# Two layers of cross-attention and FFN on one core: the first layer's softmax sums made on VectorE by 32-row transposes and additions, in place of TensorE products with ones

## Chip, cores and metric

One core of one Trainium2 chip runs one launch of the kernel. The metric is device time in microseconds, the median of the runs of a kernel; smaller is better.

## The reference, cut to what matters

All data is float32. x and the context hold 16 batches of 64 tokens with 512 features. The change touches the first layer's attention only, 32 query heads in 8 key-value heads of 128:

```
x = x + _L0_xattn_ref(_layernorm(x), ctx, ctx, mask, Wq, Wk, Wv, Wo)   # the change is in here
x = x + _L0_ffn_ref(_layernorm(x), A, B, Wr)                          # gated low-rank experts
x = x + _L1_xattn_ref(_layernorm(x), ctx, Wq, Wk, Wv, Wo)             # 16 heads of 96
x = x + _L1_ffn_ref(_layernorm(x), W, bias, A, Bf, coeffs, scales)

# in _L0_xattn_ref, per batch and head:
logits = 30.0 * jnp.tanh(einsum(q, k) * ATTN_MULT / 30.0)
logits = jnp.where(mask, logits, -1e30)
weights = jax.nn.softmax(logits, axis=-1)       # exp(logit) / sum over the 64 context tokens
attn = einsum(weights, v);  return attn @ Wo
```

## The kernel before, in words

The program is one hand-written list of steps, made by `plan()`. Every engine walks the same list and does its own part of each step, in that order, so the list is each engine's queue. Semaphores join the engines. Large products are made from float32r halves ("h" and "l"), three products for each, 12 for a tile of 512 columns.

The first layer runs in 16 units u = 0 to 15. A unit is half of the batches (8 of 16) for one key-value head, with its four query heads. Unit u does this:

- `burst(u)`: the attention's own products, together. `d0(u-2)` multiplies weights with V in two halves h, each with two PSUM tiles; `sum0(u-1)` makes sums of exponentials; `b0(u)` makes the logits of this unit, context tokens on the partitions (two batches of 64 on 128 rows), 1024 columns of queries.
- ScalarE then takes tanh and exp, GpSimd multiplies with the mask (`keep`, semaphore `masked`). The result is E0, 128x1024, in `Eb` for even u and in `pTb` for odd u.
- four projections `q0(u+1, n)` of the next unit, each with a rope: three VectorE operations (L1249, L1250, L1252, the last of which frees the PSUM bank) and an addition on GpSimd (L903). `b0(u+1)` waits for the last of these additions. In even units each is followed by `split` steps for weights: a copy by ScalarE and a subtraction by GpSimd (L880).
- four output products `e0(u-2, c)`, which VectorE adds to x (L1163). After the second stands `norm0(u-1)`: VectorE multiplies E0 with `rsum`, the reciprocal sums (L1271). `d0` of that unit waits for it.
- `k0`, the next key-value head's projection with its own rope (until unit 13), and in units 0 to 3 two V tiles, `v0`.

The sums: the context tokens lie on partitions, so TensorE multiplies E0 with `ones` (128x32), eight products of 128 columns (L1534, two instructions each) into one bank. VectorE takes the reciprocal (L1267, 128x256), SyncE writes it to the DRAM tensor `recs` with two DMAs (L827), waits for their landing, and reads it back into `rsum`, broadcast over the partitions, with two DMAs of 256 KB (L832). SyncE's queue also issues the weight loads (L804), three splits ahead of their use, in list order.

PSUM tiles without a fixed bank take the next of a ring of six banks (0, 1, 4, 5, 6, 7). A tile waits until the sixth tile before it has been read.

Around the last units the list is: unit 15 with k1(0, 0, 0), e0(13, 0), e0(13, 1), norm0(14), e0(13, 2), e0(13, 3), the splits of the last four output weights wo0 28 to 31; then k1(0, 0, 1), burst(16) with d0(14), k1(1, 0, 0), and e0(14, 0). The load of wo0 31 stands behind the split of wo0 28.

Of the kernel before, what the change touches and what calls it, by code (L numbers as in the profile page):

```python
# [7 lines left out]
NU = 16  # L8
# [54 lines left out]
def plan():  # L63
    p = Plan()
# [61 lines left out]
    def burst(u):  # L126

        if 0 <= u - 2:
            for h in range(2):
                for w in range(2):  # L130
                    tile("d0", u - 2, h, w)
                step("d0", u - 2, h)
        if 0 <= u - 1 < NU:
            stage("sum0", u - 1)
        if u < NU:
            for h in range(2):
                tile("b0", u, h, bank=2 + h)
            step("b0", u)
# [78 lines left out]
    for u in range(NU):  # L217

        def queries(n):
            if u + 1 < NU:  # L220
                q0(u + 1, n)
                if u % 2 == 0 and u + 2 < NU:
                    split("wq0", 2 * u + 4 + n)

        def outputs(c):
            if u >= 2:
                e0(u - 2, c)

        j, hf = u // 2 + 1, u % 2
        pr, m = u // 4 + 1, u % 4  # L230
        if u == 0:
            for c in range(2):
                split("wv0", 1, c)
        burst(u)
        if u == NU - 1:
            k1(0, 0, 0)
            split("wk1", 2, 0)
        queries(0)
        queries(1)
        for c in range(2):  # L240
            outputs(c)
            if u in (4, 6):
                split("wvq", u - 4 + c)
        if u:
            norm0(u - 1)
        queries(2)
        outputs(2)
        queries(3)
        outputs(3)

        wo = [2 * u - 2 + n for n in range(4)] if u % 2 else []

        def output_weight():
            if wo:
                split("wo0", wo.pop(0))

        output_weight()
        if u and j < 8:
            k0(j, hf)
            if hf and j + 1 < 8:  # L260
                split("wk0", j + 1)
        output_weight()
        if pr < 2:
            for i in range(2):
                v0(pr, 2 * m + i)
                output_weight()

        for i in {8: (0, 1, 2), 9: (3, 4, 5), 10: (6, 7)}.get(u, ()):
            vq(i)
            output_weight()  # L270
        while wo:
            output_weight()
        if u == NU - 3:
            split("wk1", 0, 0)
        if u == NU - 2:
            split("wk1", 1, 0)
            split("wv1", 0)
# [259 lines left out]
def program(nc, a, out):  # L537
# [18 lines left out]
    with ExitStack() as ctx:  # L556
# [4 lines left out]
            return ctx.enter_context(nc.semaphore(name))  # L561


        rec = sb("rec", [128, 2, 128])

        tab = sb("tab", [128, 272])
        rope = tab[:, 0:128].rearrange("p (a n) -> p a n", a=2)
        ident = tab[:, 128:256]
        mask8 = tab[:, 256:272].bitcast(u8)
        keep = sb("keep", [128, 64])  # L570
        ones = sb("ones", [128, 32])
        many = sb("many", [128, 64])
        mv = sb("mv", [128, 8, 2])
        sm = sb("sm", [128, 2, 2, 8])
# [49 lines left out]
        V1h = sb("V1h", [128, 2, 2, 2, 96], f32r)  # L624
        V1l = sb("V1l", [128, 2, 2, 2, 96], f32r)
        ropeq = sb("ropeq", [128, 2, 64])
        recs = nc.dram_tensor("recs", (2, 2, 4, 128), f32, kind="Internal").ap()
        lowtri = sb("lowtri_sb", [128, 16])
        coef = sb("coef_sb", [128, 4])
        wcol = sb("wcol", [128, 2])  # L630
# [54 lines left out]
        s_out_rec, s_in_rec = sem("rec_out"), sem("rec_in")  # L685
# [104 lines left out]
        def sync_program(e):  # L790
            sp = Lane(e)
            for kind, *k in steps:
# [20 lines left out]
                elif kind == "ctx_load":  # L813
                    h, = k
                    for c in range(4):
                        src = a["ctxT"][c * 128:(c + 1) * 128, 512 * h:512 * h + 512]
                        e.dma_start(cst[c][h], src).then_inc(s_ldc[4 * h + c], 16)
                elif kind == "x":
                    i, = k
                    e.dma_start(xs[:, i, :], a["x"][i * 128:(i + 1) * 128, :]).then_inc(s_ldx[i], 16)  # L820
                elif kind == "sum0":
                    u, = k
                    sp.wait_ge(*read("sum0", u))
                    if u:
                        sp.wait_ge(s_in_rec, 32 * u)
                    for bb in range(2):
                        e.dma_start(recs[bb].rearrange("h g x -> g h x"), rec[16 * bb:128:32, :, :]).then_inc(s_out_rec, 16)  # L827
                    sp.wait_ge(s_out_rec, 32 * (u + 1))
                    if u:
                        sp.wait_ge(s_nrm, u)  # L830
                    for bb in range(2):
                        e.dma_start(rsum[64 * bb:64 * bb + 64, :],  # L832
                                    recs[bb].rearrange("h g x -> (h g x)").unsqueeze(0).broadcast_to([64, 1024])
                                    ).then_inc(s_in_rec, 16)
                elif kind == "ffn_load":
                    sp.wait_ge(*done("b0", 15, 1))
                    e.dma_start(aw_sb, a["aw"].rearrange("p (k n) -> p k n", k=4)).then_inc(s_aw, 16)
                    e.dma_start(bcat_sb, a["bcat"]).then_inc(s_bcat, 16)
                    e.dma_start(lowtri[:, :], a["lowtri"]).then_inc(s_low, 16)
                elif kind == "weff_load":  # L840
                    sp.wait_ge(*done("b1", 7))
                    e.dma_start(w1T[:, :, :], a["w1"].rearrange("p (k n) -> p k n", k=4)).then_inc(s_w1, 16)
                elif kind == "factor_load":
                    sp.wait_ge(*done("b1", 7))
                    e.dma_start(coef[:, 0:2], a["coef"]).then_inc(s_coef, 16)
                    e.dma_start(coef[:, 2:4], a["scl"]).then_inc(s_scl, 16)
                    for c in range(2):
                        e.dma_start(ab_sb[:, c, :], a["a1"][c]).then_inc(s_ab[c], 16)
# [18 lines left out]
        def gpsimd_program(e):  # L867
            pool = Lane(e)
            for kind, *k in steps:
# [33 lines left out]
                    e.tensor_tensor(dst, dst, tmp, ALU.add).then_inc(s_radd)  # L903
                elif kind == "consts":
                    e.memset(pTb[:, 0, 0:128], 1.0).then_inc(s_one)
                    e.memset(ones[:, :], 0.0).then_inc(s_one)
                    pool.wait_ge(s_one, 2)
                    for r in range(2):
                        e.memset(ones[64 * r:64 * r + 64, 16 * r:16 * r + 16], 1.0).then_inc(s_one)
                        pool.wait_ge(s_one, 3 + r)  # L910
                elif kind == "ctx":
                    h, c = k
                    if h:
# [244 lines left out]
        def vector_program(e):  # L1158
# [6 lines left out]
            for kind, *k in steps:  # L1165
# [94 lines left out]
                    e.tensor_scalar(many[:, :], PB[b][:, 0:64], 1.0, None, ALU.min).then_inc(free[b])  # L1260
                elif kind == "sum0":
                    u, = k
                    b = bank_of("sum0", u)
                    dve.wait_ge(*done("sum0", u))
                    if u:
                        dve.wait_ge(s_out_rec, 32 * u)
                    e.reciprocal(rec[:, :, :], PB[b][:, 0:256].rearrange("p (h x) -> p h x", h=2)).then_inc(free[b])  # L1267
                elif kind == "norm0":
                    u, = k
                    dve.wait_ge(s_in_rec, 32 * (u + 1))  # L1270
# [118 lines left out]
        def tensor_program(e):  # L1389
# [12 lines left out]
                return last  # L1402

            for kind, *k in steps:
                if kind in ("k0", "q0", "v0", "vq", "e0", "sum0", "xT", "many", "k1", "v1", "b1", "c1", "e1", "weff",
                            "dense", "half", "mgT", "delta"):
                    b = bank_of(kind, *k)
                    pe.wait_ge(*opened(kind, *k))
# [105 lines left out]
                elif kind == "b0":  # L1514
# [4 lines left out]
                    for h in range(2):  # L1519
# [5 lines left out]
                                                kT[j % 2][:, 512 * hf + 64 * b8:512 * hf + 64 * b8 + 64],  # L1525
                                                qb[:, u % 2, 256 * b8:256 * b8 + 256], start=True, stop=True)
                        last.then_inc(full[2 + h])
                elif kind == "sum0":
                    u, = k
                    pe.wait_ge(s_one, 4)  # L1530
                    pe.wait_ge(s_msk, u + 1)
                    for h in range(2):
                        for c in range(4):
                            last = e.matmul(PB[b][32 * c:32 * c + 32, 128 * h:128 * h + 128], ones[:, :],  # L1534
                                            E0[u % 2][:, 512 * h + 128 * c:512 * h + 128 * c + 128], start=True, stop=True)
                    last.then_inc(full[b])
                elif kind == "d0":
                    u, h = k
                    j, hf = u // 2, u % 2
# [226 lines left out]
```

## Time and profile before

| | |
|---|---|
| median of 3 runs | 840.76 us (840.75 to 841.42) |
| the profiled execution's own time | 840.91 us |
| its span, first to last instruction | 839.0 us |
| TensorE busy | 834.1 us, 99% of the span |
| VectorE busy | 517.8 us, 62% |
| ScalarE, GpSimd busy | 370.2 us, 361.5 us |
| granted TensorE clock | 1.000 |

The span is what the trace shows; some 1.9 us of the execution lie outside it. PE is TensorE's products, PEld its weight loads (which overlap them), DVE is VectorE, ACT ScalarE, POOL GpSimd, SPq SyncE's queue of DMA issues. All start times are microseconds from the first instruction.

### The profile page before, as it was taken

How to read it: one execution, taken by the hardware profiler on the slowest of the kernel's cores; microseconds unless marked ns; L12 is line 12 of the kernel's file. 1: busy time of each engine (PE TensorE's matmuls, PEld its weight loads, DVE VectorE, ACT ScalarE, POOL GpSimd, SP SyncE). 2: the span in 40 equal slices, each digit the busy share in tenths (PEclk: the TensorE clock that was granted, in tenths of full speed). 3: DMA queues.
4: the chain of work that ended last, by engine and by line, in shares of the span. 5: the costliest groups of instructions: out<-in, count | busy, mean ns of one | idle time of the engine just before them, and what ended most of it. 6: DMA issues, size and time to landing. Idle time of an engine off the chain costs nothing.

```text
span 839.0 us, 12399 instructions
## 1 busy us (share of the span) xinstructions
PE 834.1 (99%) x4636; PEld 692.9 (83%) x4636; DVE 517.8 (62%) x979; ACT 370.2 (44%) x920; POOL 361.5 (43%) x282
## 2 busy tenths in 40 slices
PE   9999999999999999999999999999999999999998
PEld 7878888877887877877877878898998888888887
DVE  6857565666666463555666536555356667677894
ACT  6443123123113123221223143467797877787752
POOL 5677534635637324432744441012232332356442
PEclk9999999999999999999999999999999999999999
DMA  8123211311313111210311122011010200300002
GB/s 307 51 64 88 76 39 46 106 39 51 101 39 90 37 39 51 73 28 27 104 49 35 52 82 93 0 52 51 14 39 14 63 26 20 133 14 1 2 1 101
DMA packets 24891, 48.14 MB, mean 57 GB/s; under 512 B 3456, under 2 KB 4992, under 8 KB 24704
## 3 DMA queue, kind: packets, MB, share of 16 engines
q1 hardware_dynamic: 24400, 46.70, 18.4%
q8 instruction: 37, 0.61, 0.3%
q10 hardware_dynamic: 432, 0.66, 0.2%
q14 instruction: 22, 0.18, 0.1%
HBM read 45.12 MB, written 2.23 MB: 56 GB/s over the span
## 4 chain that ended last, share of the span: by engine, by line
PE 97%; POOL 2%; DMA 1%; issue 0%; ACT 0%; DVE 0%; SPq 0%; POOLq 0%; DVEq 0%
PE PB L1394 23%; PE PB L1396 22%; PE PB L1395 22%; PE PB L1619 8%; PE PB L1550 4%; PE PB L1401 3%; PE PB L1634 3%; PE PB L1524 3%; PE PB L1438 2%; PE PB L1436 2%; PE PB L1433 2%; PE PB L1534 1%; PE PB L1571 1%; DMA arena<-in_ctxT 1%; POOL qb L903 1%; PE PB L1585 0%
## 5 line engine op out<-in xcount | busy, mean ns | idle before, releaser
L903 POOL TENSOR_TENSOR qb<-qb,arena 128x512 f32<-128x512 f32 x64 | 83.8, 1309 | 146.4 <-DVE arena L1252 146.4
L1163 DVE TENSOR_TENSOR xs<-xs,PB 128x512 f32<-128x512 f32 x111 | 75.7, 686 | 96.6 <-PE PB L1396 88.4
L985 ACT ACTIVATE Oh<-PB 96x128 fp32r<-96x128 f32 (+2 forms) x236 | 79.3, 359 | 67.1 <-PE PB L1550 48.0
L1394 PE MATMUL PB<-WOh,Oh 128*128 128x512 f32 x242 | 94.5, 391 | 0.0
L1396 PE MATMUL PB<-WOh,Ol 128*128 128x512 f32 x242 | 94.3, 389 | 0.0
L1395 PE MATMUL PB<-WOl,Oh 128*128 128x512 f32 x242 | 94.2, 389 | 0.0
L1249 DVE TENSOR_TENSOR qb<-PB,ropeq 128x512 f32<-128x512 f32 x64 | 44.2, 691 | 63.6 <-PE PB L1396 63.3
L985 ACT ACTIVATE WOh<-stage 128x512 fp32r<-128x512 f32 (+1 forms) x32 | 19.2, 619 | 132.7 <-PE PB L1396 132.6
L880 POOL TENSOR_TENSOR WOl<-stage,WOh 128x512 fp32r<-128x512 f32 (+1 forms) x32 | 40.6, 1281 | 84.0 <-ACT WOh L985 63.6
L880 POOL TENSOR_TENSOR WQl<-stage,WQh 128x512 fp32r<-128x512 f32 x38 | 48.8, 1288 | 61.7 <-ACT WQh L985 61.0
L1394 PE MATMUL PB<-xTh,WQh 128*128 128x512 f32 x188 | 75.1, 399 | 0.0
L1396 PE MATMUL PB<-xTh,WQl 128*128 128x512 f32 x188 | 73.4, 390 | 0.0
L1395 PE MATMUL PB<-xTl,WQh 128*128 128x512 f32 x188 | 73.2, 389 | 0.0
L1279 DVE TENSOR_TENSOR Ol<-PB,Oh 128x512 fp32r<-128x512 f32 x64 | 39.7, 682 | 38.0 <-ACT Oh L985 37.9
L985 ACT ACTIVATE arena<-PB 128x256 f32<-128x256 f32 (+4 forms) x48 | 25.1, 524 | 66.3 <-PE PB L1396 64.9
L1363 DVE TENSOR_TENSOR Ol<-PB,Oh 64x128 fp32r<-64x128 f32 (+2 forms) x172 | 49.2, 286 | 7.0 <-ACT Oh L985 3.5
L1396 PEld LDWEIGHTS PB<-WOh,Ol 128*128 128x128 f32 x242 | 45.4, 188 | 9.5
L1394 PEld LDWEIGHTS PB<-WOh,Oh 128*128 128x128 f32 x242 | 45.4, 188 | 9.4
L1395 PEld LDWEIGHTS PB<-WOl,Oh 128*128 128x128 f32 x242 | 45.5, 188 | 9.3
L985 ACT ACTIVATE WQh<-stage 128x512 fp32r<-128x512 f32 x38 | 23.8, 631 | 61.1 <-PE PB L1396 59.5
L1126 ACT ACTIVATE Eb<-PB,sm 128x128 f32<-128x128 f32 x128 | 45.3, 366 | 8.9 <-DVE sm L1342 8.5
L1394 PEld LDWEIGHTS PB<-xTh,WQh 128*128 128x128 f32 x188 | 35.3, 188 | 12.6 <-issue 5.8
(295 smaller groups left out, 2153.2 us busy)
## 6 DMA issues: line engine op xcount, KB each, us to landing
stage<-in_wq SPq DMA_DIRECT2D x44, 256.0 KB, 2.8
stage<-in_wo SPq DMA_DIRECT2D x44, 256.0 KB, 2.6
arena<-recs SPq DMA_DIRECT2D x32, 256.0 KB, 3.9
stage<-in_wk SPq DMA_DIRECT2D x12, 256.0 KB, 2.6
xs<-in_x SPq DMA_DIRECT2D x8, 256.0 KB, 6.4
out<-xs SPq DMA_DIRECT2D x7, 256.0 KB, 2.0
arena<-in_ctxT SPq DMA_DIRECT2D x6, 256.0 KB, 6.1
stage<-in_wv SPq DMA_DIRECT2D x4, 256.0 KB, 4.2
```

Of the source, the lines that this page charges most:

```text
L880: e.tensor_tensor(lo, staged[:, n % 4, 0:cols], hi.bitcast(f32), ALU.subtract).then_inc(s_wlo)
L903: e.tensor_tensor(dst, dst, tmp, ALU.add).then_inc(s_radd)
L985: return e.activation(dst, src, ACT.Copy)
L1126: last = e.activation(Eb[:, e2, cols], PS[:, cols], ACT.Exp, bias=mx[:, bb:bb + 1], accum_out=rs[:, bb:bb + 1])
L1163: e.tensor_tensor(xs[:, i, :], xs[:, i, :], PB[b][:, :], ALU.add).then_inc(free[b])
L1249: e.tensor_tensor(dst, src, table[:, 0:1, :].broadcast_to([128, 8, 64]), ALU.mult)
L1279: e.tensor_tensor(dl, src, dh.bitcast(f32), ALU.subtract).then_inc(free[bank_of("d0", u, h, w)])
L1363: last = e.tensor_tensor(dl, PA[bank_of("d1", t, bank)][d0:d0 + rows, h], dh.bitcast(f32), ALU.subtract)
L1394: e.matmul(dst, Ah, Bh, start=(k == 0), stop=False)
L1395: e.matmul(dst, Ah, Bl, start=False, stop=False)
L1396: return e.matmul(dst, Al, Bh, start=False, stop=(k == n - 1))
L1619: last = e.matmul(PB[b][:, :], W[:, m, r], H[:, c, cols], start=(n % 12 == 0), stop=(n % 12 == 11))
```

## The change

TensorE's step `sum0` goes, and with it its PSUM tile in the ring and the constant `ones` (three small memsets). VectorE makes the sums from E0 instead: a transpose of each 32x32 block of the 128x1024 into `rsum` (used as scratch), a sum along each 32 columns (128x1024 to 128x32), four transposes of 32x32 that bring the halves of a batch side by side, one addition 64x32, one reciprocal 64x32. Each waits for the one before, but for the four transposes among themselves. The reciprocals leave with one DMA of 64 rows of 128 bytes, not two of 8 pieces of 512. The step also stands elsewhere in the list: `sum0(u)` comes right behind `norm0(u-1)` in unit u, where it was in the burst of unit u+1.

```
@@ -130,8 +130,6 @@  burst(u)
-        if 0 <= u - 1 < NU:
-            stage("sum0", u - 1)
@@ -243,6 +241,7 @@  unit u, behind outputs(0), outputs(1)
         if u:
             norm0(u - 1)
+        step("sum0", u)
         queries(2)
...
@@ SyncE
                 elif kind == "sum0":
                     u, = k
-                    sp.wait_ge(*read("sum0", u))
+                    sp.wait_ge(s_sum, 8 * (u + 1))
                     if u:
                         sp.wait_ge(s_in_rec, 32 * u)
-                    for bb in range(2):
-                        e.dma_start(recs[bb].rearrange("h g x -> g h x"), rec[16 * bb:128:32, :, :]).then_inc(s_out_rec, 16)
-                    sp.wait_ge(s_out_rec, 32 * (u + 1))
-                    if u:
-                        sp.wait_ge(s_nrm, u)
+                    e.dma_start(recs, rec[0:64, :]).then_inc(s_out_rec, 16)
+                    sp.wait_ge(s_out_rec, 16 * (u + 1))
...
@@ VectorE
                 elif kind == "sum0":
                     u, = k
-                    b = bank_of("sum0", u)
-                    dve.wait_ge(*done("sum0", u))
+                    dve.wait_ge(s_msk, u + 1)
                     if u:
-                        dve.wait_ge(s_out_rec, 32 * u)
-                    e.reciprocal(rec[:, :, :], PB[b][:, 0:256].rearrange("p (h x) -> p h x", h=2)).then_inc(free[b])
+                        dve.wait_ge(s_nrm, u)
+                    e.transpose(rsum, E0[u % 2]).then_inc(s_sum)
+                    dve.wait_ge(s_sum, 8 * u + 1)
+                    e.tensor_reduce(psum32[:, :], rsum.rearrange("p (k i) -> p k i", i=32), axis=X, op=ALU.add).then_inc(s_sum)
+                    dve.wait_ge(s_sum, 8 * u + 2)
+                    for q in range(4):
+                        e.transpose(pair[32 * (q // 2):32 * (q // 2) + 32, 32 * (q % 2):32 * (q % 2) + 32],
+                                    psum32[32 * q:32 * q + 32, :]).then_inc(s_sum)
+                    dve.wait_ge(s_sum, 8 * u + 6)
...
+                    e.tensor_tensor(rec[0:64, :], pair[0:64, 0:32], pair[0:64, 32:64], ALU.add).then_inc(s_sum)
+                    dve.wait_ge(s_sum, 8 * u + 7)
+                    e.reciprocal(rec[0:64, :], rec[0:64, :]).then_inc(s_sum)
@@ TensorE
-                elif kind == "sum0":
-                    u, = k
-                    pe.wait_ge(s_one, 4)
-                    pe.wait_ge(s_msk, u + 1)
-                    for h in range(2):
-                        for c in range(4):
-                            last = e.matmul(PB[b][32 * c:32 * c + 32, 128 * h:128 * h + 128], ones[:, :],
-                                            E0[u % 2][:, 512 * h + 128 * c:512 * h + 128 * c + 128], start=True, stop=True)
-                    last.then_inc(full[b])
```

VectorE's queue in unit 0, before: the ropes of q0(1, 1), q0(1, 2) and q0(1, 3) (from banks 5, 7 and 0), then the reciprocal of unit 0, which belongs to the burst of unit 1.

```order
L1249 TENSOR_TENSOR qb<-PB5,ropeq 128x8x64
L1250 TENSOR_TENSOR arena<-PB5,ropeq 64x512
L1252 TENSOR_TENSOR arena<-PB5,ropeq 64x512
L1249 TENSOR_TENSOR qb<-PB7,ropeq 128x8x64
L1250 TENSOR_TENSOR arena<-PB7,ropeq 64x512
L1252 TENSOR_TENSOR arena<-PB7,ropeq 64x512
L1249 TENSOR_TENSOR qb<-PB0,ropeq 128x8x64
L1250 TENSOR_TENSOR arena<-PB0,ropeq 64x512
L1252 TENSOR_TENSOR arena<-PB0,ropeq 64x512
L1267 RECIPROCAL rec<-PB6 128x256
```

The same place after the change (lines are those of the new file: 1243, 1244 and 1246 are the rope):

```order
L1243 TENSOR_TENSOR qb<-PB5,ropeq 128x8x64
L1244 TENSOR_TENSOR arena<-PB5,ropeq 64x512
L1246 TENSOR_TENSOR arena<-PB5,ropeq 64x512
L1261 STREAM_TRANSPOSE arena<-Eb 128x1024
L1263 TENSOR_REDUCE psum32<-arena 128x32
L1267 STREAM_TRANSPOSE pair<-psum32 32x32 x4
L1272 TENSOR_TENSOR rec<-pair 64x32
L1274 RECIPROCAL rec<-rec 64x32
L1243 TENSOR_TENSOR qb<-PB7,ropeq 128x8x64
L1244 TENSOR_TENSOR arena<-PB7,ropeq 64x512
L1246 TENSOR_TENSOR arena<-PB7,ropeq 64x512
L1243 TENSOR_TENSOR qb<-PB0,ropeq 128x8x64
```

The sums of unit 0 now stand between the rope of q0(1, 1) and that of q0(1, 2), ahead of the last two ropes for which b0(1) waits.

VectorE's queue in unit 1, before: norm0(0), then the ropes of q0(2, 2), q0(2, 3) and k0(1, 1); the last reads bank 4, which is the fourth bank of d0(0).

```order
L1271 TENSOR_TENSOR Eb<-Eb,arena 128x1024
L1249 TENSOR_TENSOR qb<-PB0,ropeq 128x8x64
L1250 TENSOR_TENSOR arena<-PB0,ropeq 64x512
L1252 TENSOR_TENSOR arena<-PB0,ropeq 64x512
L1249 TENSOR_TENSOR qb<-PB1,ropeq 128x8x64
L1250 TENSOR_TENSOR arena<-PB1,ropeq 64x512
L1252 TENSOR_TENSOR arena<-PB1,ropeq 64x512
L1249 TENSOR_TENSOR arena<-PB4,tab 128x512
L1250 TENSOR_TENSOR arena<-PB4,tab 64x512
L1252 TENSOR_TENSOR arena<-PB4,tab 64x512
```

After the change; k0(1, 1) is now in bank 1, again the bank that the fourth tile of d0(0) takes:

```order
L1278 TENSOR_TENSOR Eb<-Eb,arena 128x1024
L1261 STREAM_TRANSPOSE arena<-pTb 128x1024
L1263 TENSOR_REDUCE psum32<-arena 128x32
L1267 STREAM_TRANSPOSE pair<-psum32 32x32 x4
L1272 TENSOR_TENSOR rec<-pair 64x32
L1274 RECIPROCAL rec<-rec 64x32
L1243 TENSOR_TENSOR qb<-PB7,ropeq 128x8x64
L1244 TENSOR_TENSOR arena<-PB7,ropeq 64x512
L1246 TENSOR_TENSOR arena<-PB7,ropeq 64x512
L1243 TENSOR_TENSOR qb<-PB0,ropeq 128x8x64
L1244 TENSOR_TENSOR arena<-PB0,ropeq 64x512
L1246 TENSOR_TENSOR arena<-PB0,ropeq 64x512
```

Five kinds of instructions of sum0(1) now stand ahead of the two q ropes and the k0 rope (whose first instruction is the next row).

SyncE's queue at the end of the first layer, before: the sums of unit 14 (written and read), two output weights (wo0 30 and 31), three loads of V weights for the second layer, the sums of unit 15.

```order
L827 DMA recs<-rec 4x2x128 x2
L832 DMA arena<-recs 64x1024 x2
L804 DMA stage<-in_wo 128x512 x2
L804 DMA stage<-in_wv 128x384 x3
L827 DMA recs<-rec 4x2x128 x2
L832 DMA arena<-recs 64x1024 x2
L804 DMA stage<-in_wq 128x512 x2
```

After the change:

```order
L828 DMA recs<-rec 64x32
L831 DMA arena<-recs 64x1024 x2
L806 DMA stage<-in_wo 128x512 x3
L828 DMA recs<-rec 64x32
L831 DMA arena<-recs 64x1024 x2
L806 DMA stage<-in_wo 128x512
L806 DMA stage<-in_wv 128x384 x3
L806 DMA stage<-in_wq 128x512 x2
```

The first two rows are now the sums of unit 14; the three loads behind them end with wo0 30. The sums of unit 15 stand ahead of the load of wo0 31.

## Rows read from the trace of the kernel before

**Rows 1.** Page of the kernel before: busy time by engine, and the chain that ended last
```profile
PE 834.1 (99%) x4636; PEld 692.9 (83%) x4636; DVE 517.8 (62%) x979; ACT 370.2 (44%) x920; POOL 361.5 (43%) x282
...
PE 97%; POOL 2%; DMA 1%; issue 0%; ACT 0%; DVE 0%; SPq 0%; POOLq 0%; DVEq 0%
```

**Rows 2.** Timeline, TensorE's weight loads: start us, length us, engine, line, operation
```profile
200.70 0.38 PEld L1534 LDWEIGHTS PB<-pTb,ones 128*32 128x32 f32 x16 [0.33 <-issue]
201.27 1.49 PEld L1524 LDWEIGHTS PB<-qb,arena 128*64 128x64 f32 x16 [0.20 <-issue]
...
518.91 0.19 PEld L1394 LDWEIGHTS PB<-cTh,WQh 128*128 128x128 f32 x1 [0.33 <-issue]
```

**Rows 3.** VectorE by form: instruction, shapes, count, busy us, mean ns, idle before
```profile
L1267 DVE RECIPROCAL rec<-PB 128x256 f32<-128x256 f32 x16 | 28.0, 1747 | 1.4 <-PE PB L1534 1.4
...
L1342 DVE TENSOR_REDUCE sm<-PB 128x4 f32<-128x512 f32 x32 | 21.9, 685 | 30.7 <-PE PB L1634 30.7
...
L1271 DVE TENSOR_TENSOR Eb<-Eb,arena 128x1024 f32<-128x1024 f32 x8 | 9.8, 1220 | 0.0
L1350 DVE RECIPROCAL sm<-sm 128x4 f32<-128x4 f32 x32 | 5.7, 178 | 7.6 <-ACT Eb L1126 7.2
```

**Rows 4.** Timeline, VectorE, end of unit 0
```profile
50.55 0.68 DVE L1252 TENSOR_TENSOR arena<-PB,ropeq 64x512 f32<-64x512 f32 x1
51.86 0.69 DVE L1249 TENSOR_TENSOR qb<-PB,ropeq 128x512 f32<-128x512 f32 x1 [0.63 <-PE PB L1396]
```

**Rows 5.** Timeline, GpSimd, end of unit 0
```profile
54.03 1.29 POOL L903 TENSOR_TENSOR qb<-qb,arena 128x512 f32<-128x512 f32 x1 [0.17 <-DVE arena L1252]
55.28 1.30 POOL L880 TENSOR_TENSOR WQl<-stage,WQh 128x512 fp32r<-128x512 f32 x1
56.75 1.28 POOL L903 TENSOR_TENSOR qb<-qb,arena 128x512 f32<-128x512 f32 x1 [0.18 <-DVE arena L1252]
```

**Rows 6.** Timeline, TensorE, burst of unit 1
```profile
57.34 0.64 PE L1534 MATMUL PB<-Eb,ones 128*32 128x128 f32 x16
58.09 1.95 PE L1524 MATMUL PB<-qb,arena 128*64 128x256 f32 x16
```

**Rows 7.** Timeline, VectorE, unit 1
```profile
69.01 0.68 DVE L1249 TENSOR_TENSOR qb<-PB,ropeq 128x512 f32<-128x512 f32 x1
...
71.18 0.69 DVE L1249 TENSOR_TENSOR qb<-PB,ropeq 128x512 f32<-128x512 f32 x1
```

**Rows 8.** Timeline, TensorE, burst of unit 2
```profile
76.67 2.00 PE L1550 MATMUL PB<-Eb,arena 64*128 64x256 f32 x16
```

**Rows 9.** Timeline, SyncE's DMA queue, unit 15
```profile
485.69 1.17 SPq L827 DMA_DIRECT2D recs<-rec  x2
487.96 1.15 SPq L832 DMA_DIRECT2D arena<-recs  x2
489.15 0.58 SPq L804 DMA_DIRECT2D stage<-in_wo  x1
```

**Rows 10.** One load behind the sums' reads, 489.1 to 490 us: issue to landing
```profile
DMA to landing us min/median/max: 4.2/4.2/4.2
```

**Rows 11.** The sums' DMAs of unit 7, write and read: length in ns, first and last start
```profile
L827 SPq DMA_DIRECT2D recs<-rec x2: 559/563/567, 264.7 to 265.3; - x2
L832 SPq DMA_DIRECT2D arena<-recs x2: 500/548/597, 268.2 to 268.8; - x2
```

**Rows 12.** Timeline, VectorE, unit 15
```profile
493.28 1.22 DVE L1271 TENSOR_TENSOR Eb<-Eb,arena 128x1024 f32<-128x1024 f32 x1
```

**Rows 13.** Timeline, ScalarE, end of unit 15
```profile
499.68 0.62 ACT L985 ACTIVATE W<-stage 128x512 fp32r<-128x512 f32 x1
500.76 1.19 ACT L985 ACTIVATE arena<-PB 96x512 f32<-96x512 f32 x2 [0.46 <-PE PB L1396]
501.98 0.60 ACT L985 ACTIVATE Oh<-PB 128x512 fp32r<-128x512 f32 x1
```

**Rows 14.** Timeline, TensorE, first product of e0(14, 0)
```profile
506.01 0.39 PE L1394 MATMUL PB<-WOh,Oh 128*128 128x512 f32 x1
```

More of the change, by code:

```diff
@@ L561, in sem @@
             return ctx.enter_context(nc.semaphore(name))
-        rec = sb("rec", [128, 2, 128])
+        psum32 = sb("psum32", [128, 32])
+        pair = sb("pair", [128, 64])
+        rec = sb("rec", [128, 32])
         tab = sb("tab", [128, 272])
@@ L570, in program @@
         keep = sb("keep", [128, 64])
-        ones = sb("ones", [128, 32])
+        spare = sb("spare", [128, 160])
         many = sb("many", [128, 64])
@@ L626, in program @@
         ropeq = sb("ropeq", [128, 2, 64])
-        recs = nc.dram_tensor("recs", (2, 2, 4, 128), f32, kind="Internal").ap()
+        recs = nc.dram_tensor("recs", (64, 32), f32, kind="Internal").ap()
         lowtri = sb("lowtri_sb", [128, 16])
@@ L684, in program @@
         s_one, s_dup = sem("ones"), sem("many")
-        s_out_rec, s_in_rec = sem("rec_out"), sem("rec_in")
+        s_sum, s_out_rec, s_in_rec = sem("sums"), sem("rec_out"), sem("rec_in")
         s_ohi, s_ohi1 = sem("o_hi"), sem("o_hi1")
@@ L822, in sync_program @@
                     u, = k
-                    sp.wait_ge(*read("sum0", u))
+                    sp.wait_ge(s_sum, 8 * (u + 1))
                     if u:
                         sp.wait_ge(s_in_rec, 32 * u)
-                    for bb in range(2):
-                        e.dma_start(recs[bb].rearrange("h g x -> g h x"), rec[16 * bb:128:32, :, :]).then_inc(s_out_rec, 16)
-                    sp.wait_ge(s_out_rec, 32 * (u + 1))
-                    if u:
-                        sp.wait_ge(s_nrm, u)
+                    e.dma_start(recs, rec[0:64, :]).then_inc(s_out_rec, 16)
+                    sp.wait_ge(s_out_rec, 16 * (u + 1))
                     for bb in range(2):
                         e.dma_start(rsum[64 * bb:64 * bb + 64, :],
-                                    recs[bb].rearrange("h g x -> (h g x)").unsqueeze(0).broadcast_to([64, 1024])
+                                    recs[32 * bb:32 * bb + 32, :].rearrange("k j -> (k j)").unsqueeze(0).broadcast_to([64, 1024])
                                     ).then_inc(s_in_rec, 16)
@@ L905, in gpsimd_program @@
                     e.memset(pTb[:, 0, 0:128], 1.0).then_inc(s_one)
[L906 to L910, printed above, removed]
                 elif kind == "ctx":
@@ L1262, in vector_program @@
                     u, = k
-                    b = bank_of("sum0", u)
-                    dve.wait_ge(*done("sum0", u))
+                    dve.wait_ge(s_msk, u + 1)
                     if u:
-                        dve.wait_ge(s_out_rec, 32 * u)
-                    e.reciprocal(rec[:, :, :], PB[b][:, 0:256].rearrange("p (h x) -> p h x", h=2)).then_inc(free[b])
+                        dve.wait_ge(s_nrm, u)
[7 more added lines that the diff above has]
+                    dve.wait_ge(s_sum, 8 * u + 6)
+                    if u:
+                        dve.wait_ge(s_out_rec, 16 * u)
+                    e.tensor_tensor(rec[0:64, :], pair[0:64, 0:32], pair[0:64, 32:64], ALU.add).then_inc(s_sum)
+                    dve.wait_ge(s_sum, 8 * u + 7)
+                    e.reciprocal(rec[0:64, :], rec[0:64, :]).then_inc(s_sum)
                 elif kind == "norm0":
@@ L1404, in tensor_program @@
             for kind, *k in steps:
-                if kind in ("k0", "q0", "v0", "vq", "e0", "sum0", "xT", "many", "k1", "v1", "b1", "c1", "e1", "weff",
+                if kind in ("k0", "q0", "v0", "vq", "e0", "xT", "many", "k1", "v1", "b1", "c1", "e1", "weff",
                             "dense", "half", "mgT", "delta"):
```

## The prediction

> **What bounds the kernel now.** I read the page first: TensorE is busy 99% of the span and holds 97% of the chain that ended last, GpSimd 2% [rows 1]. So a microsecond taken from TensorE's queue is a microsecond of the kernel, unless TensorE then waits. The second view was the timeline around the bursts, for what the removed products cost. The third was the timeline of the other queues where they come close to TensorE: these rows decide whether the gain is kept.
>
> **What is removed.** In the burst shown, the weight loads of the sums start at 200.70 and those of b0 at 201.27 [rows 2]: 0.574 us for one `sum0`, with the pause of 0.20 that b0 has behind it. The pause of 0.33 ahead of it stays: a burst without sums shows the same 0.33 between d0(15) and the projection behind it (518.91) [rows 2]. The distance is the same in all other units and in the last; only in unit 1 b0 waited a little longer. 16 times 0.574 is **9.2 us**, about 1.1%. VectorE loses 16 reciprocals of 1.75 us [rows 3].
>
> **What is added.** The chain on VectorE is C long, per unit. No row shows its transposes. The 32-bit 128x1024 with two inputs takes 1.22 [rows 3]; I take 1.24 for the large transpose. The sum over 512 columns takes 0.685, two thirds of a microsecond; for 1024 I take 1.2, as the 1.22 of the other operation on 1024. The smallest operation takes 0.178 for 4 columns [rows 3]; 32 columns at the pace of the large ones (1.2 ns a column) add 0.03 to 0.04, so I take 0.22 for each of the four small transposes (0.88) and 0.19 for the addition. A reciprocal takes 0.178 for 4 columns and 1.747 for 256 [rows 3], 6.2 ns a column, so 0.35 for 32. Waits on the engine's own results add some 0.17. **C = 4.0 us.** Bounds: 3.4, if the small ones overlap and cost 0.15 each and the large ones 1.1 each; 5.1, if a transpose of 32-bit data takes twice a pass (2.3). Per unit VectorE does 2.3 us more, 36 us in all on 518 busy of 839: it doesn't become the bound, but it is late in places.
>
> The Trainium skill, Vector Engine (DVE) Microarchitecture Reference, section 3.8, says that the transpose is pipelined to sustain one element per cycle per lane; it gives no price for 32-bit data. No row here shows a transpose. By that rule the price is near my choice.
>
> **Where VectorE is late.** In most units it isn't seen. The chain stands behind norm0(u-1); VectorE then has some 2 us before the next rope and 2 more before the one after, and b0's last addition on GpSimd ends some 4 us ahead of b0, since e0 and k0 stand between. Three places are different, and each takes a full C or more.
>
> *Unit 0.* There is no e0 yet, so VectorE's ropes follow each other almost without a break and b0(1) waits for GpSimd: the last addition ends at 58.03, b0(1) starts at 58.09 [rows 5, 6]. Now sum0(0) stands ahead of the last two ropes. It starts when L1252 ends, 51.25 [rows 4], and ends at 55.3. The rope of q0(1, 2) starts there, not at 51.86. Its addition follows 2.17 later (54.03 less 51.86) at 57.5, then GpSimd's weight subtraction 1.25 later at 58.7, then the last addition 1.3 later at 60.0, which takes 1.28 [rows 4, 5]; b0(1) starts at 61.33. Without `sum0` TensorE is there at 57.34 [rows 6] and stands for 4.0. Against 58.09 b0(1) is **3.24 late**, and this unit's 0.574 is already in that.
>
> *Unit 1.* All times here are in the frame of before, shifts left out. sum0(1) takes the place of the rope that starts at 69.01 [rows 7] and ends at 73.1. Two q ropes follow at 2.17 each (69.01, 71.18 [rows 7]) to 77.5, then the k0 rope of 2.1, to 79.6. It frees the bank that the fourth tile of d0(0) needs. d0(0) starts at 76.67 and takes 1.9 for eight products [rows 8]; the first into the fourth bank is the sixth, near 77.8. TensorE stands **1.8 us**. With b0(2) as the only check (its addition would end just before it) this wait would be missed: it is the ring's.
>
> *Unit 15.* sum0(15) now stands ahead of the load of wo0 31 in SyncE's queue; before, it was issued right behind the load of 489.15 [rows 9], ten microseconds ahead of its use (the copy at 499.68 [rows 13]). norm0(14) ends at 494.50 [rows 12], the chain at 498.56. SyncE writes at 498.6. Before, the second write went out at 486.3 and the first read at 487.96, 1.66 later [rows 9]; so the read goes out at 500.25 and the load 1.19 later (487.96 to 489.15 [rows 9]), at 501.4. Behind 512 KB of reads it lands 4.2 later [rows 10], at 505.6. ScalarE's queue waits there: the weight's copy 0.62, the k1 tile's two copies 1.19, then the copies of d0(14), the first 0.60 [rows 13]. The second ends 0.5 later and VectorE's subtraction takes 0.69, like the sum of 512 columns: 509.4. e0(14, 0), which stood at 506.01 [rows 14], would be due at 505.44. It waits **4.0 us**.
>
> The Trainium skill, DMA: Bandwidth & Descriptors, gives a fixed cost of about 2.0 us per DMA (Anatomy of one DMA, for the other issuing path) and says that pieces under 512 bytes are read, changed and written (Specifications). The new write has pieces of 128 bytes. The row has 1.66 from issue to the next step, for pieces of 512; with the page's 2.0 the wait would be 0.3 longer. I go by the row.
>
> *Near a limit.* In unit 14 (no k0 there) the last rope is some 0.5 late where b0(15) has about 1.1 to spare, by the same views. It costs nothing up to C = 4.6 and then one for one.
>
> **Sum.** 15 units give back 8.6 (15 x 0.574). Unit 0 costs 3.24, unit 1 costs 1.8, unit 15 costs 4.0: together 9.0. Net +0.4 on the profiled 840.91, whose span of 839.0 would be 839.4: 841.3. That execution is 0.15 above the median, so the median becomes **841.2 us**. Each microsecond of C is worth 3. SyncE's earlier reads, the loads of weights in other units (three splits ahead) and the memsets that go are hidden by the same 2.7 us per TensorE tile; uncovered, a load would show as in unit 15.
>
> **Rivals.**
> - *Only b0(1) is late* (the textbook case: fewer products on the busiest engine, cover everywhere else). -8.6 + 3.24 = -5.4: 835.4. For it speaks the slack in most units; against it the two rows of waits above. Between this and the forecast: with C at 3.4 all three waits shrink by 0.6, which gives 839.4, and with the wait in unit 1 gone as well 838.2. Faster than 839.1 in all: 0.15.
> - *A 32-bit transpose takes two passes.* C = 5.1, +1.1 at three places and 0.5 in unit 14: +3.8 more, 845.0. It decides for "slower" from C = 4.4 on. For it: no row shows one; against it: all 32-bit operations in rows 3 take one pass. 0.18.
> - *The sums' way through DRAM is longer,* by the page's rule on small pieces or because the three V loads issued right behind share the engines. In unit 7, with a load in flight, the way from the second write to the read took 2.9 instead of 1.66 (265.3 to 268.2 [rows 11]). The 1.24 would fall on unit 15 alone: 842.4, slower with the smallest addition. 0.10.
> - *The forecast:* three waits eat the gain, C between 3.5 and 4.4: 839.5 to 842.4. 0.57.
>
> **Numbers.** 0.2% is 1.7 us, about what a measurement of this kernel can tell from no change: faster is under 839.1, slower over 842.4. Faster 0.15, same 0.57, slower 0.28. The range takes the bound C = 3.4 below and C = 5.1 above: 839.0 to 845.0.
>
> **What would show it.** TensorE without L1534, b0 right behind d0 with one pause of 0.33; a wait of 4.0 at b0(1) on GpSimd; 1.8 in d0(0) on VectorE's k0 rope; 4.0 at e0(14, 0) on VectorE, ScalarE or the weight wo0 31, with ScalarE's copy waiting for a DMA until near the 505th microsecond (plus the shift). The large transpose at 1.2 to 1.3 us. The forecast is wrong if the transpose or the small ones have another price, if SyncE gets through the two DMAs at another pace, or if a fourth place waits that I hold for covered.

## The result and the profile after

| | before | after |
|---|---|---|
| median | 841.09 us (4 runs, 840.75 to 841.42) | 846.23 us (4 runs, 845.58 to 848.11) |
| ratio of the runs | | 1.0065, 95% interval 1.0047 to 1.0083 |
| span of the profiled execution | 839.0 us | 844.6 us (its own time 846.75) |
| mean granted TensorE clock | 1.000 | 0.994 |

The change makes the kernel 5.1 us slower. The forecast was 841.2 us with a range to 845.0: it misses by 5.0 us, and the range by 1.2. In the four runs after the change the mean granted clock was 0.992 to 0.996.

The page of the changed kernel, the rows that answer to [rows 1]: busy time by engine, and the chain that ended last.

```profile
PE 829.8 (98%) x4380; PEld 689.6 (82%) x4380; DVE 548.5 (65%) x1091; ACT 369.1 (44%) x920; POOL 360.8 (43%) x279
...
PE 93%; DVE 2%; POOL 1%; DMA 1%; issue 1%; ACT 0%; SPq 0%; POOLq 0%; DVEq 0%
```

TensorE has 4.3 us less busy time, not 9.2, and holds 4% less of the chain. Two things must be found: where it stands (waits with nothing to do), and why its remaining products are busy for longer. The view of waits of the changed kernel names the first (what TensorE waited for: us in total, times, longest):

```profile
PE PB L1401 <- DVE Ol L1286: 5.3, 1, 5.3
PE PB L1531 <- POOL qb L902: 3.7, 1, 3.7
PE PB L1548 <- DVE arena L1246: 1.3, 1, 1.3
```

These are e0(14, 0), b0(1) and d0(0), the three places of the prediction. The second is in the view of windows of the changed kernel (stretch, its length, busy us of PE, PEld, DVE, ACT, POOL with their counts, granted clock, DMA share, GB/s):

```profile
56.00:59.20 3.20, 1.30 (x11) 1.09 (x10) 3.13 (x5) 0.67 (x2) 1.99 (x2) 1.00 0.30 87
59.30:66.00 6.70, 5.03 (x19) 2.88 (x20) 0.00 (x0) 1.80 (x3) 2.84 (x3) 0.50 0.39 113
66.10:80.00 13.90, 13.90 (x67) 11.65 (x66) 10.61 (x18) 1.91 (x4) 6.02 (x3) 1.00 0.00 1
80.00:500.00 420.00, 418.73 (x2075) 335.61 (x2076) 277.48 (x437) 105.39 (x180) 204.55 (x149) 1.00 0.21 60
506.00:509.70 3.70, 0.00 (x0) 0.00 (x0) 1.24 (x3) 3.64 (x7) 1.26 (x1) 1.00 0.22 56
509.90:513.10 3.20, 3.09 (x7) 2.48 (x8) 1.04 (x2) 1.87 (x4) 1.58 (x2) 0.50 0.03 11
513.30:520.00 6.70, 6.70 (x32) 5.52 (x31) 4.19 (x8) 0.00 (x0) 0.19 (x1) 1.00 0.44 139
```

While TensorE stands at b0(1), its clock falls to half (1.2 GHz) and stays there for 6.8 us, while b0(1) and the first products behind it run; at e0(14, 0) it falls just before the wait ends and stays for 3.4. In the profiled execution of the kernel before, the clock is whole to the last instruction. The Trainium skill, TensorE: Matmul & The Clock Gate, Part 1, says that the array's clock is at 1.2 GHz after idleness and that activity brings 2.4 GHz back; these rows agree, with 0.50 from 59.3 to 66.0 behind the stand and 1.00 afterwards.

The starts of the same products in both kernels, from their timelines, give the account. Each line is the distance between the starts of the two steps' first products, in us; "wait" and "half clock" say what most of the difference is:

| from, to | before | after | difference |
|---|---|---|---|
| b0(0) to b0(1) | 16.64 | 19.63 | +3.0, wait |
| b0(1) to d0(0) | 18.58 | 20.99 | +2.4, half clock |
| d0(0) to b0(2) | 2.50 | 3.88 | +1.4: wait 1.95, sum0 gone 0.57 |
| b0(2) to b0(15) | 403.05 | 395.45 | -7.6: 13 times sum0 |
| b0(15) to d0(14) | 18.43 | 18.42 | 0 |
| d0(14) to e0(14, 0) | 5.36 | 10.30 | +4.9: wait 5.5, sum0 gone 0.57 |
| e0(14, 0) to d0(15) | 10.97 | 12.56 | +1.6, half clock |
| d0(15) to the end | 321.99 | 322.04 | 0 |

b0(0) itself comes 0.1 earlier. Together +5.6 us, the difference of the spans. Without the two lines of half clock it would be +1.6.

The added instructions, VectorE of the changed kernel by form, have the sizes that were assumed:

```profile
L1263 DVE TENSOR_REDUCE psum<-arena 128x32 f32<-128x1024 f32 x16 | 19.5, 1220 | 0.5
L1267 DVE STREAM_TRANSPOSE pair<-psum 32x32 f32<-32x32 f32 x64 | 12.9, 201 | 2.0
...
L1261 DVE STREAM_TRANSPOSE arena<-pTb 128x1024 f32<-128x1024 f32 x8 | 10.0, 1246 | 0.8
...
L1274 DVE RECIPROCAL rec<-rec 64x32 f32<-64x32 f32 x16 | 5.5, 345 | 0.6
L1272 DVE TENSOR_TENSOR rec<-pair 64x32 f32<-64x32 f32 x16 | 2.9, 183 | 0.5
```

Timelines of the changed kernel at b0(1), against [rows 4 to 6]: VectorE, GpSimd, TensorE (start, length, then in brackets the idle time and what ended it).

```profile
51.15 1.25 DVE L1261 STREAM_TRANSPOSE arena<-Eb 128x1024 f32<-128x1024 f32 x1
...
55.11 0.62 DVE L1243 TENSOR_TENSOR qb<-PB,ropeq 128x512 f32<-128x512 f32 x1
...
57.21 1.26 POOL L902 TENSOR_TENSOR qb<-qb,arena 128x512 f32<-128x512 f32 x1 [3.46 <-DVE arena L1246]
...
59.66 1.26 POOL L902 TENSOR_TENSOR qb<-qb,arena 128x512 f32<-128x512 f32 x1
...
60.97 3.68 PE L1531 MATMUL PB<-qb,arena 128*64 128x256 f32 x16 [3.67 <-POOL qb L902]
```

VectorE's chain of sums occupies 51.15 to 55.11, so the rope of q0(1, 2) and the two additions on GpSimd come late one after the other. And b0(1)'s sixteen products take 3.68, where [rows 6] has 1.95.

Timelines of the changed kernel at e0(14, 0), against [rows 9, 13, 14]: SyncE's queue, ScalarE, TensorE.

```profile
497.71 0.47 SPq L828 DMA_DIRECT2D recs<-rec  x1
499.92 1.09 SPq L831 DMA_DIRECT2D arena<-recs  x2
501.06 0.58 SPq L806 DMA_DIRECT2D stage<-in_wo  x1
501.69 1.38 SPq L806 DMA_DIRECT2D stage<-in_wv  x3
...
505.96 0.63 ACT L979 ACTIVATE W<-stage 128x512 fp32r<-128x512 f32 x1 [7.13 <-DMA stage<-in_wo]
...
510.01 0.76 PE L1401 MATMUL PB<-WOh,Oh 128*128 128x512 f32 x1 [5.32 <-DVE Ol L1286]
```

From the write to the read pass 2.21 us (1.66 assumed), from the load's issue to ScalarE's copy 4.90 (4.2), from the copy to e0(14, 0) 4.05 (3.8): the links are the predicted ones, each longer. The first two vary between executions, as v_loads_later and late_first_two show below.

### The profile page after: what moved, and what is told of

It is laid out like the page before. It is cut to its first block, busy times and chain, and to the rows that moved or that the text cites. A ratio compares the mean times of both kernels' runs of the same rounds, so it can differ in the third digit from the quotient of the medians.

```text
span 844.6 us, 11969 instructions
## 1 busy us (share of the span) xinstructions
PE 829.8 (98%) x4380; PEld 689.6 (82%) x4380; DVE 548.5 (65%) x1091; ACT 369.1 (44%) x920; POOL 360.8 (43%) x279
## 4 chain that ended last, share of the span: by engine, by line
PE 93%; DVE 2%; POOL 1%; DMA 1%; issue 1%; ACT 0%; SPq 0%; POOLq 0%; DVEq 0%
PE PB L1401 22%; PE PB L1403 21%; PE PB L1402 21%; PE PB L1617 8%; PE PB L1531 4%; PE PB L1408 3%; PE PB L1632 3%; PE PB L1548 3%; PE PB L1445 1%; PE PB L1443 1%; PE PB L1440 1%; PE PB L1569 1%; DMA arena<-in_ctxT 1%; POOL qb L902 1%; DMA stage<-in_wo 1%
```

## The experiments

The kernels were measured in three groups of four, each group on one chip together with the kernel before (its medians there: 841.59, 841.05 and 841.02 us). The ratio of each kernel is against the kernel before of its own group. Where a distance is given, as +16.64 for b0(1), it is the one of the table above, read from that kernel's trace.

### Is it the clock? Fill the waits

**fill_waits.** Products that nobody reads where TensorE stands, into an unused bank pair ahead of b0(1)'s wait, and into its own bank, once that is open, ahead of e0(14, 0)'s products:

```
+                    if u == 1:
+                        pe.wait_ge(*opened("b0", u, 0))
+                        for _ in range(16):
+                            e.matmul(PB[2][:, :], cTh[:, 0, 0:128], cTh[:, 0, 0:512], start=True, stop=True)
...
+                    if k == [14, 0]:
+                        for _ in range(22):
+                            e.matmul(PB[b][:, :], cTh[:, 0, 0:128], cTh[:, 0, 0:512], start=True, stop=True)
```

> TensorE does products on constant data while it waits: 16 of 512 columns ahead of b0(1), 22 ahead of e0(14, 0); they write banks that the real products overwrite. The waits' ends don't move. If the granted clock falls because TensorE stood idle there (theory A), both stretches at 1.2 GHz go (6.8 and 3.4 us long after the change) and the span falls by about 4: 842.2 us, clock 1.000. If the clock fell for another reason (rival: the sums' products are gone, or the chip), the time stays at 846.

Measured: 846.21 us, ratio 1.0055 (1.004 to 1.007), not the expected 842.2. The clock was 1.000 in the profiled execution and one other, 0.998 in two. The first filling does what it should: b0(1) comes at +19.73, as late as in the change, and b0(1) to d0(0) takes 18.61, not 20.99. e0(14, 0) to d0(15) takes 10.97, not 12.56. But the second filling had a wait of its own, in the view of waits of fill_waits, and then ran past the load, so that e0(14, 0) came 2.0 later:

```profile
PE PB L1561 <- ACT arena L979: 2.2, 1, 2.2
```

This shows the clock's share at the first place; the total says nothing, because of the second filling. The next kernel mends it.

**fill_clean.** The second filling goes ahead of the opening of the bank, 20 products into the unused pair:

```
+                    if [kind, *k] == ["e0", 14, 0]:
+                        pe.wait_ge(*read("b0", 15, 0))
+                        for _ in range(20):
+                            e.matmul(PB[2][:, :], cTh[:, 0, 0:128], cTh[:, 0, 0:512], start=True, stop=True)
```

> The change with TensorE kept at work in its two long waits by products that nobody reads, in the third bank pair: 16 of 512 columns ahead of the wait of b0(1), and now 20 ahead of the opening of e0(14,0)'s bank (in fill_waits the second filling waited for that bank itself and ran past the load). Theory that the fallen clock took the missing time: b0(1) and e0(14,0) start where they do in the changed kernel, the granted clock stays 1.000, and the stretches behind them give back 2.4 and 1.6 us: 4.0 less, about 842.2 us. Rival, that the stretches behind the waits are long for another reason (late buffers): the intervals b0(1) to b0(2) and e0(14,0) to d0(15) stay 24.9 and 12.6 us and the time stays at 846 us.

Measured: 842.52 us (11 runs, all with clock 1.000), ratio 1.0016 (1.0008 to 1.0025), which lies below the interval of the change (1.0047 to 1.0083). Windows of fill_clean, over both places, columns as above:

```profile
40.00:70.00 30.00, 29.90 (x168) 24.12 (x167) 16.48 (x28) 12.16 (x21) 19.17 (x14) 1.00 0.21 62
490.00:520.00 30.00, 29.69 (x140) 23.68 (x140) 15.57 (x27) 7.44 (x14) 7.03 (x6) 1.00 0.29 88
```

b0(1) starts at the same distance (19.72), the stretch behind it takes 18.58 and the one behind e0(14, 0) 11.05: 3.9 us come back by giving TensorE useless work. (e0(14, 0) came 0.5 earlier too, with a quicker landing of the load, 4.6 for 4.9, and a write-to-read time of 1.98; b0(0) came 1.0 later in this execution.) The kernel's real work and its order are the same, so the long stretches behind the waits are the clock and not late buffers: the rival is refuted.

### Are these three waits all? Move what causes them

**load_ahead.** The load of wo0 31 stands ahead of sum0(15) in the list:

```
+    early, late = ("load", "wo0", 31), ("sum0", NU - 1)
+    ordered.remove(early)
+    ordered.insert(ordered.index(late), early)
```

> The load of wo0 31 stands ahead of sum0(15) in SyncE's queue, nothing else moves. Theory A (three places, each with its wait): the wait of 5.3 to 5.7 us at e0(14, 0) goes and the 1.2 GHz stretch behind it: 5.5 + 1.6 = 7.1 less, 839.1 us; the other two waits stay at 3.9 and 1.7. Rival (VectorE is too full everywhere, the last wait only shows it): e0(14, 0) still waits for VectorE, 845 or more.

Measured: 839.85 us (10 runs), ratio 0.998 (0.9971 to 0.999). d0(14) to e0(14, 0) takes 4.82, the old 5.36 less sum0, and the stretch behind it 10.97. One load's place in SyncE's queue was worth some 6 us. The wait of 3.7 at b0(1) is still there, and the ten executions split by what follows it: five with mean clock 0.998 took 838.57 to 840.10 us (median 839.56), five with 0.996 took 839.50 to 841.30 (median 840.68).

**late_first_two.** Only the sums of units 0 and 1 move, to the end of their units, behind the ropes:

```
-        step("sum0", u)
+        if u > 1:
+            step("sum0", u)
...
+        if u < 2:               # behind the unit's last step
+            step("sum0", u)
```

> sum0(0) and sum0(1) stand at the end of their units, behind all ropes; the others stay. Theory A: the waits at b0(1) (3.9) and in d0(0) (1.7) go, and the 6.8 us at 1.2 GHz, of which TensorE worked 4.9 and lost 2.4: b0(1) starts near 58.1 again. 3.2 + 1.7 + 2.4 = 7.3 less: 838.9 us, with the wait at e0(14, 0) left. Rival (VectorE too full): the delay moves to burst 1 and 2, 843 or more.

Measured: 839.17 us, ratio 0.996 (0.9946 to 0.9975). b0(1) is back at +16.64, d0(0) at +18.57, b0(2) at +1.93. What is left is the tail, waits and windows of late_first_two:

```profile
PE PB L1405 <- DVE Ol L1290: 4.3, 1, 4.3
```
```profile
500.70:504.00 3.30, 2.80 (x7) 2.25 (x8) 1.44 (x3) 2.27 (x5) 1.29 (x2) 0.50 0.17 66
```

**both_moves.** Both edits at once; the sums of units 2 to 15 stay where the change has them in VectorE's queue, that of unit 15 with the load ahead of it in SyncE's.

> The change with both moves at once: the sums of units 0 and 1 at the end of their units (late_first_two) and the load of wo0 31 queued on SyncE ahead of sum0(15) (load_ahead); the sums of units 2 to 14 stay where the change has them. Theory, that three waits and the half clock behind them are all that the change costs: in late_first_two's execution the stretch to e0(14,0) takes 9.25 us and the one behind it 12.43, in load_ahead's 4.82 and 10.97, so 5.9 less than its span of 835.7: a span near 829.8 and about 833.3 us, as old_place (833.7) or a little below it. Rival, that old_place is fast for another reason, the place of the other 13 sums: the time stays above 835.3 us.

Measured: 832.41 us, ratio 0.9894 (0.9878 to 0.9911), clock 1.000. So the three waits and the half clock behind two of them are the whole cost of the new place: the other 13 sums cost nothing there, and the rival is refuted.

**old_place.** The VectorE sums, but `sum0(u-1)` back in burst u:

```
+        if 0 <= u - 1 < NU:     # in burst(u), between d0 and b0
+            step("sum0", u - 1)
-        step("sum0", u)         # in unit u
```

> The sums on VectorE as in the change, but the step stands where it was, in burst(u+1) between d0(u-1) and b0(u+1). This is the engine's change alone, without the move. Theory A: TensorE loses 16 x 0.574 = 9.2 and gains no wait but one below 0.5 us at d0(15), whose norm0 then waits for the sums' way through DRAM: 832.5 to 833.5 us. Rival (the work on VectorE costs, wherever it stands): 840 or more.

Measured: 833.7 us, ratio 0.9906 (0.9892 to 0.9921), 0.2 above the expected range: the wait at d0(15) is 1.0, not below 0.5, and 15 sums pay, not 16. The arithmetic of the change is a gain; the place lost it.

### What of the tail's length? The loads behind the load

**v_loads_later.** The three V loads wait in SyncE's queue for the landing of wo0 31:

```
+                    if k == ["wv1", 1]:
+                        m = splits["wo0", 31]
+                        sp.wait_ge(s_stage[m % 4], 16 * (m // 4 + 1))
```

> The change with the three loads of wv1 (1 to 3), which SyncE issues right behind the load of wo0 31, held until that load has landed. Theory, that the load's 4.88 us (against 4.2 in the kernel before) came from sharing the DMA queues with these three: it lands about 0.7 us earlier after its issue and e0(14,0) starts 0.7 earlier, the time is about 845.5 us. Rival, that they are not the cause: it takes 4.9 us again, the time stays at 846.2 us, or above it, if the V loads are now themselves late.

Measured: 845.32 us, ratio 1.0055 (1.0042 to 1.0068). From issue to landing in the same stretch (490 to 512 us), first the changed kernel, then v_loads_later; the last number is us:

```profile
stage<-in_wv SPq DMA_DIRECT2D x3, 192.0 KB, 4.7
...
stage<-in_wo SPq DMA_DIRECT2D x1, 256.0 KB, 4.9
```
```profile
stage<-in_wv SPq DMA_DIRECT2D x3, 192.0 KB, 2.5
...
stage<-in_wo SPq DMA_DIRECT2D x1, 256.0 KB, 4.2
```

That looks like the expectation, but it isn't shown. In late_first_two the three V loads are issued right behind the load of wo0 31, as in the change, and its landing (485 to 502 us of that trace) is the short one all the same:

```profile
stage<-in_wv SPq DMA_DIRECT2D x3, 192.0 KB, 4.1
...
stage<-in_wo SPq DMA_DIRECT2D x1, 256.0 KB, 4.1
```

With the V loads right behind it, this load took 4.88, 4.27, 4.62, 4.14 and 4.41 us in the traces of the changed kernel, fill_waits, fill_clean, late_first_two and double_turn; with them held, 4.17. The write-to-read time varies too: 2.21, 1.80, 1.98, 1.91 and 1.68 in the same five, 1.93 with the V loads held. So d0(14) to e0(14, 0) takes 9.26 in late_first_two and 9.31 in v_loads_later, where the profiled execution of the changed kernel has 10.30. The medians differ by 0.9 us, but the intervals overlap. What made the changed kernel's execution slower here stays open. The clock also behaved otherwise than in the changed kernel, windows of v_loads_later:

```profile
61.90:65.20 3.30, 3.30 (x13) 1.98 (x10) 0.00 (x0) 2.33 (x4) 0.11 (x1) 0.50 0.03 6
...
505.60:512.30 6.70, 4.38 (x10) 3.48 (x11) 2.48 (x4) 4.06 (x9) 2.26 (x3) 0.50 0.47 130
```

The short stretch now follows b0(1)'s wait (3.7 us, as before) and the long one belongs to e0(14, 0), though its wait is shorter (4.3, not 5.3).

### Does VectorE's work cost anything elsewhere? Double it

**double_old.** old_place, with the large transpose done twice:

```
+                    e.transpose(rsum, E0[u % 2]).then_inc(s_twice)
+                    dve.wait_ge(s_twice, u + 1)
                     e.transpose(rsum, E0[u % 2]).then_inc(s_sum)
```

> The kernel of old_place with the large transpose done twice in each unit: 16 times 1.28 = 20.5 us more work on VectorE, about 1.3 us later in each unit. Theory, that VectorE's added work costs only where TensorE waits for VectorE: one wait is left there, d0(15) for norm0(15), and grows by 1.3 us; near-limits add at most as much again: 833.7 + 1.3 = 835.0 us, at most 836.3. Rival, that the added work costs a part of its length in every unit (VectorE as a hidden bound): several microseconds more, up to 854.

Measured: 834.9 us, ratio 0.9932 (0.9919 to 0.9944). Some 20 us more of VectorE's time cost 1.2 us, and one wait grew by 1.1. The rival is refuted. Waits of old_place, then of double_old, and the window behind it:

```profile
PE PB L1549 <- DVE pTb L1279: 1.0, 1, 1.0
```
```profile
PE PB L1552 <- DVE pTb L1282: 2.1, 1, 2.1
...
511.30:514.60 3.30, 3.30 (x16) 2.41 (x16) 3.16 (x7) 1.09 (x2) 0.00 (x0) 0.50 0.06 23
```

This profiled execution, which had half clock behind its wait of 2.1, took 836.59, and another with the same mean clock of 0.998 took 835.79. The other three had a mean clock of 1.000 and took 834.60 to 834.90.

**double_turn.** The same doubling in the change, where the sums stand ahead of the ropes.

> The change, its sums where it has them, with the large transpose done twice in each unit (1.28 us more in front of each reciprocal). Theory, that the sum costs only where TensorE waits for VectorE: b0(1) 1.3 later, d0(0) no more than now beyond it, b0(15) late by some 0.7 in unit 14, e0(14,0) 1.3 later: 3.3 us more, 849.5 us, up to 850.8, and up to 4 us beyond that where the longer waits bring longer stretches at half clock. Rival, that VectorE's work costs in each unit: 20 us more, 866.

Measured: 853.94 us, ratio 1.0147 (1.0132 to 1.0162): 7.7 above the change, between the expectation's 850.8 and the 4 us beyond it. Waits and windows of double_turn:

```profile
PE PB L1404 <- DVE Ol L1289: 6.3, 1, 6.3
PE PB L1534 <- POOL qb L903: 5.6, 2, 4.9
PE PB L1551 <- DVE arena L1247: 2.3, 2, 1.4
```
```profile
61.50:68.30 6.80, 5.53 (x21) 3.25 (x22) 0.00 (x0) 2.31 (x4) 2.44 (x2) 0.50 0.35 99
88.90:92.20 3.30, 3.30 (x16) 1.68 (x16) 0.00 (x0) 1.73 (x4) 3.30 (x4) 0.50 0.41 101
515.50:522.20 6.70, 5.63 (x13) 4.46 (x14) 2.08 (x5) 2.84 (x6) 1.97 (x2) 0.50 0.42 110
```

One term of it was wrong: d0(0) to b0(2) grew by 1.5, where nothing more was expected; that unit 1's own sum is 1.3 longer as well explains it. b0(1) came 1.28 later and b0(15) 0.67, as said, e0(14, 0) 0.95, where 1.3 was said. A third stretch of half clock came in unit 2, behind the wait in d0(0), and the one in the tail is 6.8, not 3.4. The rival of 866 is far off.

### The best place

**best_place.** old_place, but unit 15's sum ahead of burst 16's first step:

```
-        if 0 <= u - 1 < NU:
+        if 0 <= u - 1 < NU - 1:
             step("sum0", u - 1)
...
+    step("sum0", NU - 1)        # ahead of burst 16
```

> The kernel of old_place, but with unit 15's sum queued on VectorE ahead of burst 16's first step and not within that burst, so that norm0(15) is earlier. Theory: the last wait, d0(15) for norm0(15), which was 1.0 us there, goes, and the time is 833.7 - 1.0 = 832.7 us. Rival: the sum is then ahead of work that TensorE needs just as soon (the evictions of k1(0,0,1)), the wait only moves, and the time stays at 833.7 us or above.

Measured: 832.99 us, ratio 0.9906 (0.9891 to 0.9921); the wait for norm0(15) is gone (d0(15) at +10.97, not 12.01). The ratio is that of old_place, so both were run again, side by side.

> The kernel of old_place once more, beside best_place on one chip: 833.7 us. Its remaining wait, d0(15) for norm0(15), is 1.0 us.

> The kernel of best_place once more, beside old_place on one chip. If the last wait, 1.0 us at d0(15), was worth its length: 1.0 us below old_place_again, about 832.7 us. Rival: the two are equal within 0.3 us.

Measured: old_place 833.49 us (833.14 to 833.67), ratio 0.9906 (0.9891 to 0.9921); best_place 832.22 us (831.95 to 832.49), ratio 0.9891 (0.9876 to 0.9906). On one chip, with ranges that don't touch, best_place is 1.3 us faster; its trace has 1.2 less ahead of d0(15). It and both_moves are 8.6 to 8.8 us faster than the kernel before, about 1.1%: 15 times 0.574 is 8.6, since the sixteenth, ahead of b0(1), gives nothing at either place (+16.64, where GpSimd is the limit).

## Why the prediction was wrong

- **What is removed** was right: 13 units give 7.6 us, 0.585 each (0.574 said), and the whole is there in both_moves and best_place.
- **What is added** was right: 1.246, 1.220, 4 times 0.201 at 0.23 between starts, 0.183 and 0.345, C = 3.96 to the start of the next rope in unit 0 (4.0 said). The rival of two passes for a 32-bit transpose (2.3 us) falls. VectorE's busy time rose by 30.7 us, where 36 was said, since C holds the waits between its instructions too. The Trainium skill, Vector Engine (DVE) Microarchitecture Reference, section 3.8, has one element per cycle and lane; 1.246 for 1024 columns beside 1.22 for an operation with two inputs agrees.
- **Unit 0**: 3.24 said, 3.0 measured. **Unit 1**: 1.8 said, 1.95 measured, at the ring's bank. **Near a limit**: unit 14 costs nothing (b0(14) to b0(15) takes 25.80 for 26.38, which is sum0 less); in double_turn it waits 0.7, as said for a longer C.
- **Unit 15** was right in its mechanism and too small: 4.0 said, 5.5 measured in the profiled execution. 0.55 is the write's way to the read (2.21 for 1.66), 0.7 the load's landing (4.88 for 4.2), 0.25 the copies. Other executions with the same order of the tail have 4.5 (late_first_two) and 5.0 (fill_clean), so up to 1.0 of the 1.5 varies from one execution to the next. The rival "DRAM way is longer" got 0.10 for a cost that comes on top of the forecast's waits. Its two causes aren't shown: the load lands in 4.14 with the V loads right behind it as well (late_first_two), and the way to the read is short in most units. The Trainium skill, DMA: Bandwidth & Descriptors, gives about 2.0 us fixed per DMA (Anatomy of one DMA, for the other issuing path) and a penalty for pieces under 512 bytes (Specifications). The single write with its pieces of 128 bytes had 1.68 to 1.73 to the read in 14 of the 16 units, 1.91 and 2.21 in units 13 and 15, and the kernel before, with pieces of 512, had 1.64 to 1.68 in 12 units and 1.84 to 2.89 in four: neither a penalty nor the 2.0 shows here.
- **Sum.** The lower end of the range was set at 839.0, where its own working has 839.4 for C = 3.4; nothing hangs on it. The step that failed is that a wait was priced at its own length. "8.6 less, 9.0 more" has no term for what TensorE does after it has stood: two of the three waits are followed by half clock, 2.4 and 1.6 us. That is 4.0 of the 5.2 by which the sum missed (+5.6 measured, +0.4 said); the tail's 1.5 is the rest, less some 0.3 elsewhere. With a whole clock the change takes 842.5 (fill_clean), 1.3 above the forecast. No rival had the clock either, though the list of waits gave reason to ask: all of [rows 1 to 14] come from a kernel in which TensorE's longest wait is 1.0 us, so they can't show what a longer stand costs. Its view of waits:

```profile
PE PB L1443 <- POOL ones L906: 1.0, 1, 1.0
PE PB L1433 <- ACT cTh L985: 1.0, 2, 0.6
```

## What to carry to other kernels

When a change makes a busy TensorE stand for some microseconds in one piece, its price can be the wait plus a stretch at half clock: here 3.0 + 2.4 and 5.5 + 1.6 us. A step that leaves the busiest engine for an idle one still has a place in three queues: here the place made a difference of 14 us (846.2 against 832.2), and the cure was not less work but two sums behind the ropes and one load ahead of a wait (both_moves, 832.4). Look at the first units, the last unit, and each DMA queued behind a step that waits for a round trip.

## What the runs showed of the hardware

- The clock of TensorE fell during or behind waits of 3.7 to 6.3 us, in one trace 1.2 us after the wait had ended (v_loads_later), and stayed at half for 3.4 or 6.8 us, most of it in full work. Which of the two follows wasn't fixed by the wait: after the same 3.7 at b0(1) it was 6.8 in the change and 3.4 in v_loads_later.
- Among shorter waits the outcome differed. Waits of 1.0 and 1.1 (old_place, old_place_again), of 1.3 (the change, at d0(0)) and of 2.2 (fill_waits) were not followed by half clock in their traces; one of 2.1 (double_old) was, and so were two of 0.8 and 1.4 close together in d0(0) of double_turn.
- The time of a kernel with such a wait goes with its clock. late_first_two took 837.82, 837.99 and 839.17 us at a mean clock of 0.998 and 839.34 and 839.53 at 0.996; double_old splits alike, load_ahead in its medians (839.56 and 840.68), with ranges that overlap. The clock isn't the whole spread: the 11 runs of fill_clean, all at 1.000, go from 841.64 to 843.51.
- Three loads of 192 KB issued right behind 512 KB of reads and a load of 256 KB landed 4.1 to 4.7 us after their issue, in five traces. Held until that load had landed (v_loads_later) they took 2.4, 2.5 and 3.4.
